# Eight GpSimd drains among the scatter-adds of a mixture-of-experts block

## The reference, cut to what matters

```python
x = x + xattn(layernorm(x), ctx)          # 2 x 1024 tokens of 256, 16 heads, 154 keys
gate = softmax(layernorm(x) @ Wg + bg)    # 8 experts, the best 2 of each token
for e in range(8):
    h = gelu(xn @ W1[e] + b1[e])          # 256 -> 1024
    y = h @ W2[e] + b2[e]                 # 1024 -> 256
    output = output + y * combine_w[..., e:e + 1]
x = x + output
```

## Time and profile before

| what | value |
|---|---|
| runs | 425.68, 431.43, 430.43 us |
| median | 430.43 us |
| span of the profiled execution (first to last instruction) | 422.9 us |
| median less that span | 7.5 us |
| mean granted TensorE clock | 0.980 |
| busy: TensorE, VectorE, ScalarE, GpSimd | 385.5, 318.1, 217.8, 186.6 us |

### The profile page before, as it was taken

How to read it: one execution, slowest core, us unless ns; L and a number is a source line. 1 busy time by engine, 2 the same in 40 slices (tenths; PEclk the granted TensorE clock), 3 DMA queues, 4 the chain that set the end, 5 groups by cost and what they waited for, 6 DMA issues and landing times.

```text
span 422.9 us, 15170 instructions
## 1 busy us (share of the span) xinstructions
PE 385.5 (91%) x4834; PEld 300.9 (71%) x4834; DVE 318.1 (75%) x989; ACT 217.8 (52%) x587; POOL 186.6 (44%) x273
## 2 busy tenths in 40 slices
PE   4868999999999989999999999999999999999960
PEld 3746777766677777777787877877787777778740
DVE  6576998979888877854788989776777777777760
ACT  2445786767777756645384444444443444444420
POOL 3300267777776666554543333233233333333341
PEclk9997999999999999999999999999999999999995
DMA  8648867777788654237233563332332333333210
GB/s 278 135 118 253 241 198 231 221 232 207 231 239 231 189 196 139 91 78 250 64 54 66 95 121 52 52 49 36 51 45 40 47 45 47 45 53 47 28 15 0
DMA packets 73441, 50.88 MB, mean 120 GB/s; under 512 B 48400, under 2 KB 67472, under 8 KB 73232
## 3 DMA queue, kind: packets, MB, share of 16 engines
q1 hardware_dynamic: 66168, 41.44, 36.1%
q0 software_dynamic: 7152, 8.47, 11.8%
q10 hardware_dynamic: 48, 0.01, 0.0%
HBM read 28.52 MB, written 17.37 MB: 109 GB/s over the span
## 4 chain that ended last, share of the span: by engine, by line
PE 63%; DVE 14%; issue 7%; POOL 6%; DMA 5%; ACT 1%; SPq 1%; ACTq 0%; DVEq 0%; POOLq 0%
PE ps L1264 59%; POOL rs L569 3%; DVE mx L925 3%; DVE wts L910 3%; DMA out<-stage,row_id 2%; POOL rs L571 2%; DMA area<-qd 2%; PE ps L1408 2%; PE ps L1402 2%; DVE xn L855 1%; DMA area<-in_x 1%; PE ps L1423 1%; DVE area L1179 1%; DVE nbT L1069 1%; DVE st L974 1%
## 5 line engine op out<-in xcount | busy, mean ns | idle before, releaser
L1264 PEld LDWEIGHTS ps<-stage,wts 128*128 x1872 | 130.8, 98 | 40.5 <-issue 2.0
L1264 PE MATMUL ps<-stage,wts 128*128 128x128 f16 x1872 | 155.2, 219 | 1.3 <-issue 1.3
L1264 PE MATMUL ps<-wts,area 128*128 x624 | 150.3, 327 | 0.1
L808 ACT ACTIVATE area<-ps,late 128x128 f32<-128x128 f32 x312 | 89.1, 371 | 114.5 <-PE ps L1264 111.5
L628 POOL DMA_INDIRECT out<-stage,row_id x39 | 69.0, 1770 | 129.7 <-DVE stage L1212 74.6
L1264 PE MATMUL ps<-area 128*128 128x128 f16 (+5 forms) x784 | 61.2, 226 | 6.8 <-DMA area<-qd 3.8
L1177 DVE TENSOR_SCALAR area<-area 128x512 f16<-128x512 f32 x78 | 33.7, 432 | 42.7 <-ACT area L808 39.6
L925 DVE TENSOR_REDUCE mx<-ps 128x3 f32<-128x462 f32 (+1 forms) x96 | 53.3, 577 | 12.8 <-PE ps L1264 12.8
L1264 PEld LDWEIGHTS ps<-area 128*128 128x128 f16 (+1 forms) x784 | 45.4, 101 | 18.5 <-issue 7.8
L1179 DVE SCALAR_TENSOR_TENSOR area<-area 128x512 f16<-128x512 f32 x78 | 54.8, 702 | 2.7
L671 ACT ACTIVATE area<-ps 128x512 f32<-128x512 f32 x80 | 47.0, 601 | 17.3 <-PE ps L1264 14.5
(11 more groups left out here) (131 smaller groups left out, 413.4 us busy)
## 6 DMA issues: line engine op xcount, KB each, us to landing
stage<-in_w SPq DMA_DIRECT2D x32, 512.0 KB
area<-qd SPq DMA_DIRECT2D x16, 256.0 KB, 4.0
qd<-wts SPq DMA_DIRECT2D x48, 64.0 KB, 2.1
area<-in_x SPq DMA_DIRECT2D x16, 128.0 KB, 3.3
out<-area SPq DMA_DIRECT2D x16, 128.0 KB
xlist<-pad_rows SPq DMA_DIRECT2D x15, 130.0 KB, 3.7
area<-nbT SPq DMA_DIRECT2D x64, 1.0 KB
area<-in_b SPq DMA_DIRECT2D x1, 1024.0 KB, 8.7
```

Of the source, the lines that this page charges most:

```text
L808: last = nc.scalar.activation(h32[par][:, c * P:(c + 1) * P], h_ps[par][m][:, f * P:(f + 1) * P], ACT.Gelu_apprx_tanh, bias=b1T[:, ds(numb ...
L1264: return nc.tensor.matmul(out_, lhsT, rhs, start=start, stop=stop, skip_group_check=skip)
```

## The change

A tuple of eight block numbers is added, and after the scatter-add of each of these blocks GpSimd executes a drain.

```diff
@@ -28,6 +28,7 @@
 LAST = NT + 2
+RETIRED = (3, 8, 13, 18, 23, 28, 33, 35)
 GROUPS = [(0, 3), (3, 3), (6, 2), (8, 3), (11, 3), (14, 2)]
@@ -646,6 +647,9 @@
             for t in range(2, NBLK):
                 add_block(t)
+                if t in RETIRED:
+
+                    pool.drain()
             pool.wait_ge(s.added, 16 * NBLK)
```

## The result

The changed kernel takes 421.19 us (median of 20 runs, 417.70 to 426.64), the kernel before 425.91 us (20 runs, 423.33 to 431.43). The two medians lie 4.7 us apart. The ratio, taken without the executions that fell in the chip's slower state, is 0.988, with a 95% interval of 0.9853 to 0.9908: 5.1 us gained, between 3.9 and 6.3, where 5.2 were forecast. The median before was 430.43 when only three runs stood behind it; with twenty it is 4.5 us lower, which is why the forecast of 425.2 us lies 4 us above the measured time though the gain is right.

What follows compares the result with a forecast made beforehand. TensorE bounds the experts, GpSimd and its DMAs the tail, then GpSimd's end drain alone. Saving 5.46 us there and losing 0.25 after block 35 gives -5.2 us: 430.43 to 425.2 us, range 420.0 to 431.0.

Steps and rivals of the forecast that it cites:

- The bound, and the place of the gain: TensorE's own work sets the time until 395 us, GpSimd and its DMAs the tail; 5.87 us of end drain on the path.
- What the long drain does: GpSimd's last drain walks over 71 DMAs not yet retired, at 0.080 us each plus at most 0.174 us fixed.
- the line through two points: Drain price drawn from GpSimd's start drain (0.174 us, no DMA) and end drain (5.871 us, 71 DMAs).
- The end's drain: At the program's end, three DMAs left: 0.41 us in place of 5.87, 5.46 us saved, all on the path.
- The drain after block 3: 36 DMAs, 3.06 us from the writing of the descriptors; block 4's scatter-add 0.4 us late, costed at nothing.
- the cover: Time a scatter-add may be late before VectorE's `weigh` waits for its buffer: 4.3 us, read at block 33.
- The six drains with five DMAs: After blocks 8 to 33: 0.57 us each, at most 0.25 us behind the landing, under the cover; costed at nothing.
- The drain after block 35: In the tail, two DMAs, no cover: ends up to 0.25 us after the landing, 0.25 us lost straight to the end.
- Rival 1: The early drains cost the end's drain nothing; it keeps 5.87 us: 430.4 to 430.7 us, chance 0.09.
- Rival 2: Each drain walks over everything issued so far; block 36's scatter-add comes 5.6 us late: 436.0 us, chance 0.04.
- Rival 3: A drain has a large fixed part, 1.123 us as TensorE's: 3.4 us gained, 427.0 us, chance 0.07.

Runs made afterwards that it cites:

- the drain behind the last landing: The kernel before, no drain in its loop, with one drain written out behind the wait for the last landing: ratio 1.0031 (0.9979 to 1.0083).
- the drain after 35: The changed kernel with only the drain after block 35 left in its loop: ratio 0.9862 (0.9767 to 0.9957) to the kernel before.

## Why the prediction was right

**The bound, and the place of the gain.** Right. TensorE's stretch over the experts is 202.8 to 203.2 us in every version, and all of the gain is in the tail.

**What the long drain does.** Right in its form: in this kernel the line through two points now stands on eight, all DMAs landed: 0.040 us for none, 0.122 for 1, 0.292 for 3, 0.455 for 5, 0.699 for 8, 1.522 for 18, 2.910 for 35 and 5.87 for 71. The slope is 0.082 us (forecast 0.080), the fixed part 0.045 (at most 0.174). The 12 ns that the Trainium skill (VectorE: DVE Perf Modes, The DRAIN you can't avoid) gives for such drains holds for SyncE's 0.013 us and misses GpSimd's even when it is empty; at the end of the kernel before, those of ScalarE, VectorE and TensorE took 0.814, 0.393 and 1.123 us.

**The end's drain.** 5.58 us saved, forecast 5.46.

**The drain after block 3.** The cost was right, nothing for TensorE. The size of the delay and the cover were not. The forecast had block 4's scatter-add 0.4 us late. Its result was ready at 233.56 us, so that it could have started at 234.39, and it started at 237.50: 3.1 us late. Half of that is the landing of block 3's, which came 3.67 us after the writing, not 2.4 as in the execution before; with no drain in the loop at all (the drain behind the last landing) it took 3.84 us at the same block, so this isn't the drain's doing. The other half, 1.55 us, is the drain's: from landing to start 2.38 us went by in place of 0.83. The second half of the drain, 1.5 us for 36 DMAs, comes behind the landing, where the forecast had the whole under the flight.

The late scatter-add then landed late too. The windows run from its start to its landing, in the kernel before and in the changed one, in the columns of the earlier trace rows:

```profile
234.37:238.61 4.24, 4.24 (x51) 3.29 (x50) 4.01 (x16) 1.99 (x8) 1.68 (x1) 1.00 0.47 62
```
```profile
237.50:243.34 5.84, 5.84 (x73) 4.60 (x71) 4.58 (x17) 2.28 (x8) 1.59 (x1) 1.00 0.78 191
```
It took 5.84 us in place of 4.24, in a stretch in which the DMAs moved 191 GB/s in place of 62. In the five executions with a drain over 36 DMAs it took 5.0 to 5.9 us, in the seven others 3.7 to 4.2. That the traffic is the reason isn't tested.

The cover had been read at the other end of the stretch, 4.3 us. At this end the trace before has 3.2: block 4's scatter-add landed at 238.61 us, and `weigh(6)` started at 241.84. It didn't hold. VectorE waited 0.54 us at block 6's buffer (0.96 and 1.10 in two of the four other executions with such a drain, nothing in the other two), although its waits were forecast for the tail alone. The forecast had TensorE stand still next, and it didn't: it had slack of its own, which no sum of the forecast contains. So this term came out right in part by luck; it is the step that came nearest to failing.

**The six drains with five DMAs.** 0.24 us behind the landing, forecast at most 0.25; nothing on TensorE. The agreement is luck: the forecast's 0.25 was the fixed part and one DMA, whatever the number behind it, and what comes behind the landing is half of the walk, 0.045 + 5 x 0.041 = 0.25 here and 1.5 for 36 DMAs.

**The drain after block 35.** 0.15 us (0.98 against 0.83 from landing to start), forecast 0.25 by the same term.

**The rivals.** Rival 1 fell with the written-out drain: the program's own last one took 0.040 us. With it goes the rule of the Trainium skill (PSUM — Partial Sum Buffer, Engine vs sequencer instructions) that a drain waits for the engine to go idle, as an account of its price: with GpSimd idle and all DMAs landed a drain took 5.87 us. Rival 2 fell with the drain after 35, whose successor took 0.3 us. Rival 3 fell with the fixed part of 0.045 us.

**The number.** The forecast time, 425.2 us, was 4.0 us too high. The median of three runs that it was taken from was 4.5 too high, and the medians moved by 4.7 us in place of 5.2. The time alone couldn't have told the forecast from rival 1, since three runs before lay 5.75 us apart; the ratio and the rows of the last drain do.

## What to carry to other kernels

Look at what each engine does after its last counted instruction: a span that ends in an empty stretch hides its cost in sequencer rows that the busy times leave out. In this kernel a GpSimd drain costs by the number of DMAs that the engine issued since its last one (all of 128 rows of about 1 KB), so look for such a drain on the path and split the walk over places where GpSimd waits anyway, early enough that a late scatter-add is caught up before the end. A delay that never stalls TensorE can still come out at the end of a chain which has no slack of its own. And read a cover at the place where it is needed: here it was 3.2 us at block 4 and 4.3 at block 33.

## What the runs showed of the hardware that was not expected

Half of a drain's price, 0.041 us a DMA, can lie under the flight of the DMA ahead of it, and the other half came behind its landing in every run; the formula fits every drain that stood directly behind a scatter-add to 0.02 us. An explicit wait for the landing ahead of the drain brings both halves behind it (0.446 us in place of 0.24 for five DMAs).
